# Softmax denominators of one row tile in eight: a sum taken on VectorE in place of ScalarE's accumulator, and a normalisation step two half-steps later

## The reference, cut to what matters

```python
xn = _layernorm(x)                                   # x: 8 x 1024 x 512, float32
q, k, v = xn @ Wq.T, xn @ Wk.T, xn @ Wv.T             # 16 heads of 32
attn = softmax(einsum('bhsd,bhtd->bhst', q, k) * scale, axis=-1)
attn = attn + rel_bias                                # the bias comes after the softmax
s = einsum('bhst,bhtd->bhsd', attn, v)                # heads put together, then:
s = (s - mu) * rsqrt(var + 1e-5) * gamma + beta       # layer norm over 512
g = silu(spiking feed-forward of xn)
out = x + s * g
```

## Time and profile before

| | us |
|---|---|
| median of the runs | 3676.3 |
| lowest and highest of three | 3675.13, 3678.26 |
| the profiled execution | 3674.0 |
| its span, first to last instruction | 3672.2 |

### The profile page before, as it was taken

The page is one execution under the profiler, slowest core; times in us unless marked ns, Lnnn a source line. Parts: engine busy times, 40 slices in busy tenths (PEclk is TensorE's granted clock), DMA queues, the critical chain, the costliest instruction groups (busy, mean ns, idle before and its releaser), DMA issues.

```text
span 3672.2 us, 55309 instructions
## 1 busy us (share of the span) xinstructions
PE 3474.0 (95%) x20204; PEld 1475.0 (40%) x20204; DVE 2733.0 (74%) x4090; ACT 2623.7 (71%) x3917; POOL 1575.7 (43%) x898
## 2 busy tenths in 40 slices
PE   3999999999999998799999999999999999999985
PEld 1444444444444443334334343343343433434331
DVE  5366666666766667877787887887888888788786
ACT  4233333333333332799999999999999999999994
POOL 1000000000000000266777778677776777777867
PEclk6999999999999999899999999999999999999997
DMA  4011111111111111313223133232232222323221
GB/s 174 30 42 41 42 41 41 41 42 41 50 62 41 41 41 35 92 42 92 76 81 117 59 92 105 76 112 69 86 111 76 87 93 82 93 84 90 82 76 64
DMA packets 141405, 260.90 MB, mean 71 GB/s; under 512 B 19248, under 2 KB 52784, under 8 KB 140624
## 3 DMA queue, kind: packets, MB, share of 16 engines
q1 hardware_dynamic: 141136, 257.37, 22.1%
HBM read 155.77 MB, written 59.83 MB: 59 GB/s over the span
## 4 chain that ended last, share of the span: by engine, by line
ACT 36%; issue 10%; PE 7%; DVE 6%; POOL 1%; DMA 0%; ACTq 0%; SPq 0%; DVEq 0%; POOLq 0%
ACT recurrence_or_probs L1078 19%; ACT s_sb L1085 17%; DVE s_sb L1136 3%; PE misc L955 2%; PE acc L1030 2%; PE s_ps L999 2%; PE s_ps L1013 1%; DVE gate_or_tokens L1222 1%; POOL recurrence_or_probs L1329 1%; DVE nat L1170 1%; DMA xT<-xnT 0%; DVE outT L1155 0%; PE misc L938 0%; DVE recurrence_or_probs L90 0%; DVE frs L1212 0%
## 5 line engine op out<-in xcount | busy, mean ns | idle before, releaser
L1136 DVE TENSOR_SCALAR_CACHE_REDUCE s_sb<-s_ps 128x1024 f32<-128x1024 f32 x1024 | 1243.8, 1221 | 373.0 <-PE s_ps L999 338.6
L1329 POOL TENSOR_TENSOR recurrence_or_probs<-recurrence_or_probs,toep 128x2048 f32<-128x2048 f32 (+3 forms) x384 | 1321.6, 3461 | 275.6 <-ACT recurrence_or_probs L1078 275.6
L1085 ACT ACTIVATE s_sb<-s_sb,nmax 128x1024 f32<-128x1024 f32 x1024 | 1195.1, 1167 | 11.3 <-DVE s_sb L1136 11.1
L1078 ACT ACTIVATE recurrence_or_probs<-s_ps 128x1024 f32<-128x1024 f32 x1024 | 1058.7, 1035 | 16.8 <-PE s_ps L1013 16.6
L434 PE MATMUL ps_fc<-xnT_part,w_fc 128*128 128x512 f16 x3072 | 706.1, 380 | 1.4 <-DVE xnT_part L573 1.4
L447 PE MATMUL ps_y<-w_pr,hid_part 128*128 128x512 f16 x3072 | 704.5, 379 | 0.0
L514 ACT ACTIVATE relu<-ps_fc 128x512 f32<-128x512 f32 x256 | 152.8, 597 | 733.2 <-PE ps_fc L434 733.2
L999 PE MATMUL s_ps<-kst,qst 96*128 96x512 f16 x2048 | 613.9, 381 | 52.8 <-ACT recurrence_or_probs L1078 43.8
L1013 PE MATMUL s_ps<-qst,kst 99*128 99x512 f16 x2048 | 616.2, 383 | 2.4 <-DMA qst<-sub_rows 0.8
L1364 POOL MEMSET unit<- 128x16 f32 x1 | 0.1, 111 | 1408.3 <-POOLq L329 1408.3
L1030 PE MATMUL acc<-recurrence_or_probs,val 128*32 128x512 f32 x4096 | 547.4, 607 | 14.8 <-POOL recurrence_or_probs L1329 11.0
(11 more groups left out here) (117 smaller groups left out, 2537.6 us busy)
## 6 DMA issues: line engine op xcount, KB each, us to landing
toep<-table_rows SPq DMA_DIRECT2D x32, 2048.0 KB, 8.1
qst<-nat SPq DMA_DIRECT2D x384, 64.0 KB, 2.0
kst<-nat SPq DMA_DIRECT2D x384, 64.0 KB, 2.0
x_in<-in_x SPq DMA_DIRECT2D x16, 1024.0 KB, 7.4
xnT<-xnT_part SPq DMA_DIRECT2D x32, 512.0 KB, 4.2
gate<-gate_or_tokens SPq DMA_DIRECT2D x16, 1024.0 KB, 4.3
xT<-xnT SPq DMA_DIRECT2D x32, 512.0 KB, 9.2
x_or_gate<-gate SPq DMA_DIRECT2D x64, 256.0 KB, 2.8
```

Source lines behind the costliest of these rows:

```text
L1078: nc.scalar.activation(prob[:, k % PROBS, 2 * second:2 * second + 2, :].rearrange("p j n -> p (j n)"), s_ps[:, item_buffer(pair_item(m)), ...
L1085: nc.scalar.activation(s_sb[:, i % 4, :], s_sb[:, i % 4, :], ACT.Exp, bias=nmax[:, par, j, st:st + 1], scale=-1.0, accum_out=den[:, par, j ...
L1136: nc.vector.tensor_scalar(s_sb[:, i % 4, :], s_ps[:, item_buffer(tile_item(n)), :], -1.0, None, ALU.mult, ALU.min, accum_out=nmax[:, par, ...
L1329: nc.gpsimd.tensor_tensor(tile, tile, toep[:, par, :, at:at + width], ALU.add).then_inc(biased, 1)
```

## The change

Of the row tiles, those whose number in the group is a multiple of eight (0, 8, 16, 24, so 4 in 32 and 128 in 1024) are exponentiated by ScalarE without `accum_out`. VectorE sums them from `s_sb` into the same column of `den` with a `tensor_reduce` (`add_up`). It does so at the half-step three after the tile's `row_max`, which is h = 1, 9, 17 and 25, straight after that half-step's `row_max` and ahead of the other work. A new semaphore `added` counts these sums: `ln_sums` waits for it, and so does the `row_max` that overwrites such a tile's buffer, which is the very next `row_max`. Apart from that, the second and fourth `finish_normalise` move from h = 21 to h = 23.

```diff
-NORMALISE = ({19: 0, 21: 1}, {19: 2, 21: 3})
+NORMALISE = ({19: 0, 23: 1}, {19: 2, 23: 3})
...
+ADDED, ADDED_LAG = 8, 3
...
+            def tile_earlier(self, h):
+
+                n = self.g * 32 + h + AHEAD - ADDED_LAG
+                return (n // 32, n // 32 % 2, n % 32) if 0 <= n < NG * 32 else None
...
+        def summed_by_vector(i):
+
+            return i % ADDED == 0
...
-                nc.scalar.activation(s_sb[:, i % 4, :], s_sb[:, i % 4, :], ACT.Exp, bias=nmax[:, par, j, st:st + 1], scale=-1.0,
-                                     accum_out=den[:, par, j, st:st + 1]).then_inc(sum_done, 1)
+                if summed_by_vector(i):
+                    nc.scalar.activation(s_sb[:, i % 4, :], s_sb[:, i % 4, :], ACT.Exp, bias=nmax[:, par, j, st:st + 1],
+                                         scale=-1.0).then_inc(sum_done, 1)
+                else:
+                    nc.scalar.activation(s_sb[:, i % 4, :], s_sb[:, i % 4, :], ACT.Exp, bias=nmax[:, par, j, st:st + 1], scale=-1.0,
+                                         accum_out=den[:, par, j, st:st + 1]).then_inc(sum_done, 1)
...
+                act.wait_ge(added, (G * 32 + half * 16 + 16) // ADDED)
...
+                if n >= 4 and summed_by_vector((i - 4) % 32):
+                    dve.wait_ge(added, (n - 4) // ADDED + 1)
...
+            def add_up(G, par, i):
+                n = G * 32 + i
+                j, st = i % 16 // 4, i // 16 * 4 + i % 4
+                dve.wait_ge(sum_done, n + 1)
+                nc.vector.tensor_reduce(den[:, par, j, st:st + 1], s_sb[:, i % 4, :], AX, ALU.add).then_inc(added, 1)
...
                         row_max(tiles[0], tiles[1], tiles[2] + second)
+                    earlier = s.tile_earlier(h)
+                    if earlier and summed_by_vector(earlier[2]):
+                        add_up(*earlier)
                     take_misc(b, hg, s, h)
```

More of the change, by code:

```diff
@@ L703, in attention @@
         sum_done = sem("sum_done")
+        added = sem("added")
         ln_done = sem("ln_done")
```

## The result

| | before | after |
|---|---|---|
| median of the runs, us | 3677.3 | 3702.0 |
| lowest and highest of four, us | 3675.13, 3679.47 | 3701.71, 3707.24 |
| span of the profiled execution, us | 3672.2 | 3699.9 |

The changed kernel is slower: its time is 1.0071 of the time before, 95% interval 1.0053 to 1.0088. Forecast were 3683 us and a range up to 3701. The time is that of the first rival, full exclusion at h 23 (3700).

The account below looks back on a forecast made before the run. ScalarE was taken to bound the kernel, with VectorE close behind at h 17 to 28. Even slots 4.5 + odd slots 0.9 - first batch 1.5 + ahead 2.5 + last slot 0.7 = +7.1 us: forecast 3683, range 3664 to 3701.

Parts of the forecast that it names:

- the first rival: At h 23 GpSimd's product gets between the normalisation's two instructions, 1.0 us longer; +24 us, 3700; chance 0.25.
- What bounds: Main slots: ScalarE, busy 2058.47 of 2068.00 us, sets the beat; VectorE runs close behind between h 17 and h 28.
- What leaves ScalarE: Sums without accumulator lose only the read row: 0.094 us a tile, 12.0 us in 128 tiles, at most 29.
- The rival of the dear accumulator: ScalarE's accumulator costs more than its read row, 0.23 us a tile; 3666 us, between 3663 and 3674; chance 0.15.
- The reduction: VectorE's sum of 128 x 1024: 1.14 us, 1.26 where the next `row_max` waits for it; bounds 0.57 and 1.38.
- The walk up to h 23: VectorE in an even slot from h 17: a 0.5 us wait at h 20, the 0.32 at h 23 gone.
- The moved normalisation: VectorE at h 23: 1.45 us alone plus 0.3 for small GpSimd operations it meets, bounds 0 and 1.0.
- the head: Stretch 1486 to 1528 us, ahead of the main slots: two reductions on the path, 2 x 1.26 = +2.5 us.
- the tail: Last slot: `gated` of the fourth tile waits for the later normalisation, last three bias additions start later; +0.7 us.
- Ahead and behind: Outside the main slots: +2.5 us from reductions ahead of them, +0.7 from the later normalisation in the last slot.
- the first batch's -1.5: Four slots of the first batch have no normalisation and keep their gain: 4 x 0.38 = -1.5 us.

Follow-up runs that it names:

- no_reduction_21: Changed kernel without the VectorE sums: 128 tiles exponentiated without accumulator, denominators set to one, second normalisation at h 21; 3669.4 us.
- move_only: Kernel before with only the second normalisation moved from h 21 to h 23, no reductions; 3677.2 us.
- sum_21: Changed kernel with its sums on VectorE but the second normalisation left at h 21; 3685.3 us.
- narrow_gate_after: Changed kernel with GpSimd's two gate instructions on 8 of the 512 columns, the rest of the gating left out; 3671.7 us.
- gate_quarters: Changed kernel with each gated product of 128x512 on GpSimd made in four pieces of 128 columns; 3682.4 us.

## Why the prediction was wrong, step by step

**What bounds** was right: ScalarE's beat, with VectorE's stretch of h 17 to 28 as the place where it is lost.

**What leaves ScalarE** was right: 1.04 from start to start, 12.0 us in all, no shorter exponential. The rival of the dear accumulator is out. What the prediction didn't see is that even this gain is cut to 7.5 us when nothing is added (no_reduction_21).

**The reduction** was sized at 1.14 plus 0.12 for the wait. At h 1, where the next instruction doesn't wait for it, it takes 1.13 from start to start. But from its start to a `row_max` that waits for it it is 1.37 (2770.24 to 2771.61), not 1.26: the wait for its end adds 0.23. That is 0.11 more than assumed at each of h 17 and h 25. The reduction at h 9, put at nothing, cost nothing: the odd half from h 6 to 22, with reductions at h 9 and 17, is 32.72 with them and without (no_reduction_21). Those at h 1 no run has alone.

**The walk up to h 23** held. Counted from the tile of h 17, the `row_max` of h 20 was to end after 9.50 us, and did after 9.60; that of h 23 was to give way to the normalisation after 14.81, and did after 14.88. The wait at the sum of h 20 was to be 0.5 and is 0.60; the 0.32 at h 23 went.

**The moved normalisation is the step that failed**: "I take 0.3 for the small GpSimd operations it meets, bounds 0 and 1.0". The true price is 0.90 in an even slot, close to the upper bound, and 1.20 in an odd one, beyond it. The reason given for 0.3, that the first instruction is in ahead of the product, was true by the rows (2783.97 against 2784.12). It didn't lead where I took it: the normalisation is two instructions, the product (in an odd slot a small subtraction with the product behind it) stands waiting when the first ends, and the second then waits for all of it. The earlier trace rows showed this very order, product and second instruction at 1.70 and 1.63. They should have outweighed a head start of tenths, and the rival should have had the larger chance. The Trainium skill (SBUF — State Buffer, "Who interferes with whom") has it that the wait is for a whole GpSimd instruction; by that rule, the traces agree (1.65 for 0.75 against a product of 1.27; 0.83 against a piece of it). It also lets a `tensor_reduce` run undisturbed, and the 128 rows of after agree: 1206 to 1217 ns, with a bias addition of GpSimd beside most of them.

**What follows from it** came as the rival had it. It worked out +0.83 for an even slot and +0.8 for an odd one. Measured are 0.92 (0.32 + 0.60) and 0.95 (-0.17 + 1.12). Both sums count fourteen even slots, and thirteen have the loss: in the slot of group 30 there is no `take_qk` that a late normalisation could delay. That the rival's total of 3700 lies 2 us beside the time is in part luck: the head was sized 1.9 too high, the tail 1.6 too low, and 2.0 us are waits that it didn't have. The small rest in a slot is in two places: the reduction's 0.11, and in each wait, for a row that says `[0.56 <-PE s_ps L1024]` stands 1.79 us behind the one ahead, where 1.13 is the beat: 0.66 is lost. An ACT row begins some 0.1 before the one ahead ends, and the wait that is shown leaves that out.

**Ahead and behind.** The head was to lose 2.5 and lost 0.6 to the second logarithm (31.45 for 30.54, and -0.3 ahead of the first). Of the first batch's -1.5, -1.2 came. The tail was to lose 0.7 and lost 2.3, by the mechanism named. GpSimd of after, last slot:

```profile
3654.78 1.28 POOL L1342 TENSOR_TENSOR gate_or_tokens<-gate_or_tokens,x_or_gate 128x512 f32<-128x512 f32 x1 [5.02 <-DVE gate_or_tokens L1249]
...
3657.37 11.45 POOL L1356 TENSOR_TENSOR recurrence_or_probs<-recurrence_or_probs,toep 128x512 f32<-128x512 f32 x4
```

The product waits 5.02 us for the later normalisation, and the bias additions stand behind it in the queue. move_only's tail, 78.2 us, has the same.

**The range.** Its upper end, 3701, lay 1 us above the rival's 3700. Since the rival's own terms had bounds too (the reduction's wait, the tail, a collision of 1.2 instead of 1.0), its range had to reach to some 3710 by my estimate.

## What to carry to other kernels

A job of two instructions isn't covered by its first one's head start: look at what the other engine has waiting when the first ends, and take the rows where the two did meet as the price. Extra work on an engine with idle time is free or dear by its place alone, so walk from the engine's waits: sums of 128 tiles moved to VectorE cost 9 us in one set of places, those of 96 tiles brought 7 in another. A disturbance that costs nothing today (move_only, even slots) becomes a loss once such work has used up the reserve, and a collision that a margin of 0.2 us keeps away today (its odd slots) can come with it. When a GpSimd or VectorE step is moved, look for zero-width neighbours, and follow the DMA queue that waits for it.

## What was unexpected of the hardware

A reduction's successor on the same engine that waits for it starts 0.23 us later than one that doesn't (1.37 for 1.13 or 1.14 us behind the reduction's start); behind elementwise instructions it was 0.12 in the earlier trace rows.

A normalisation instruction that meets a longer GpSimd instruction waits longer. In the last slot of after, beside bias additions of 128x2048 (five in 23.31 us, 4.66 in the mean), VectorE shows:

```profile
3625.13 3.82 DVE L1246 SCALAR_TENSOR_TENSOR gate_or_tokens<-gate_or_tokens,fmv,gamma_row 128x512 f32<-128x512 f32 x1
3628.99 4.88 DVE L1249 SCALAR_TENSOR_TENSOR gate_or_tokens<-gate_or_tokens,frs,beta_row 128x512 f32<-128x512 f32 x1
```

At a new batch PE waits for the transfer of `xT`, and how long differs from kernel to kernel with no pattern that I found: 0.2 us in all before, 2.0 after, 5.2 in sum_21, 1.3 in move_only, 3.4 in narrow_gate_after. In PE's timeline of sum_21 the largest is

```profile
1690.50 1.60 PE L966 MATMUL misc<-xT,w_q 128*128 128x512 f16 x6 [1.98 <-DMA xT<-xnT]
```

and the half slot around it takes 36.14 us for 32.72. The first logarithm's start varied too, 1514.1 in after and 1519.6 in gate_quarters, although the two have the same instructions up to there. 1.0 us of it comes in the weight preparation, the rest in the two preparing slots behind 1440 us, where TensorE's granted clock is not 1.00 (0.71 and 0.87 in the stretches 1480 to 1500 and 1500 to 1530 of after, 0.67 and 0.84 in gate_quarters) and falls at other moments: the first twelve `misc<-xT,w_k` products behind 1458 us take 2.76 us in after and 5.30 in gate_quarters. Such one-off delays are a few us of a span, and the reason that distances between repeated instructions compare kernels more finely here than their times do.
